# Other order tables and another start for a one-core transformer kernel

## What is computed

```python
h = _L0_tok_ref(x, L0_tok_W)                   # patches times a matrix
h = jnp.concatenate([h, txt], axis=1)
h = h + _L0_attn_ref(_layernorm(h), ...)       # softmax over tokens, circular correlation (by DFT), projection
h = h + _L0_ffn_ref(_layernorm(h), ...)        # 192 -> 768, gelu, 768 -> 192
h = h + _L1_attn_ref(_layernorm(h), ...)       # attention over own 324 and 196 shared tokens
h = h + _L1_ffn_ref(_layernorm(h), ...)        # four experts take the 162 best tokens each, then an attention
                                               # over 324 tokens beside a gelu layer, and the results are gated
```

## Time and profile before

| what | value |
|---|---|
| median of 3 executions | 2089.15 us (2087.38 to 2093.47) |
| the profiled execution | 2096.61 us, span 2094.9 us |
| PE busy | 1871.9 us, 89% of the span |
| DVE / ACT / POOL busy | 60% / 53% / 14% |
| mean granted TensorE clock | 0.965 of full speed |

### The profile page before, as it was taken

How to read it: one execution, slowest core, us unless ns; L and a number is a source line. 1 busy time by engine, 2 the same in 40 slices (tenths; PEclk the granted TensorE clock), 3 DMA queues, 4 the chain that set the end, 5 groups by cost and what they waited for, 6 DMA issues and landing times. The chain is left out here.

```text
span 2094.9 us, 41506 instructions
## 1 busy us (share of the span) xinstructions
PE 1871.9 (89%) x11904; PEld 1260.5 (60%) x11904; DVE 1247.5 (60%) x3509; ACT 1110.8 (53%) x2583; POOL 289.3 (14%) x441
## 2 busy tenths in 40 slices
PE   3788998998998998998998997868999999999996
PEld 2565665675665675665675664435666666666664
DVE  2256566666566566666676674535767666666563
ACT  1244555555554555555555554445556565666663
POOL 4201111111111111111111110100100011001000
PEclk9799999999999999999999998879999999999998
DMA  4202212212212212212212202202433334333331
GB/s 151 68 16 58 69 32 71 64 32 74 61 32 67 64 36 69 67 34 69 65 36 69 68 27 76 75 17 80 103 100 90 87 93 119 82 101 101 100 86 36
DMA packets 161303, 143.61 MB, mean 69 GB/s; under 512 B 32284, under 2 KB 136488, under 8 KB 161064
## 3 DMA queue, kind: packets, MB, share of 16 engines
q1 hardware_dynamic: 157448, 136.69, 24.1%
q0 software_dynamic: 2304, 4.79, 1.0%
q10 hardware_dynamic: 1440, 0.75, 0.1%
HBM read 82.79 MB, written 50.16 MB: 63 GB/s over the span
## 5 line engine op out<-in xcount | busy, mean ns | idle before, releaser
L944 ACT ACTIVATE prob<-sps 108x324 f32<-108x324 f32 x1536 | 621.3, 439 | 506.6 <-PE sps L1356 470.3
L1214 DVE TENSOR_REDUCE mxh<-mps 108x1 f32<-108x324 f32 x1152 | 519.7, 489 | 319.2 <-PE mps L1390 315.4
L1356 PE MATMUL sps<-qpack,kpack 128*108 128x324 bf16 x1536 | 436.3, 318 | 33.5 <-ACT prob L944 25.6
L1390 PE MATMUL mps<-kpack,qpack 96*108 96x324 bf16 x1728 | 391.1, 296 | 46.7 <-DMA kpack<-scr_k 28.9
L1356 PEld LDWEIGHTS sps<-qpack,kpack 128*108 128x108 bf16 x1536 | 189.7, 127 | 228.2 <-ACT prob L944 163.0
L1371 PE MATMUL aps<-prob,v 128*32 128x324 f32 x3072 | 320.0, 460 | 2.4 <-DVE gmall L1202 1.1
L1390 PEld LDWEIGHTS mps<-kpack,qpack 96*108 96x108 bf16 x1728 | 215.8, 131 | 175.8 <-issue 57.6
L1342 PE MATMUL lin<-yT,w 128*128 128x324 f32 x576 | 184.0, 450 | 18.3 <-ACT g L844 14.1
L1214 DVE TENSOR_REDUCE mxs<-mps 108x2 f32<-108x392 f32 x288 | 160.0, 555 | 53.9 <-PE mps L1390 53.7
L1342 PEld LDWEIGHTS lin<-yT,w 128*128 128x128 f32 x576 | 102.4, 192 | 64.4 <-issue 33.2
L767 POOL CAST piece<-rest 128x324 bf16<-128x324 f32 x96 | 43.7, 456 | 700.2 <-DVE rest L1045 695.9
(11 more groups left out here) (150 smaller groups left out, 2354.8 us busy)
## 6 DMA issues: line engine op xcount, KB each, us to landing
qpack<-scr_q SPq DMA_DIRECT2D x96, 243.0 KB, 3.2
kpack<-scr_k SPq DMA_DIRECT2D x96, 121.5 KB, 3.3
scr_q<-piece SPq DMA_DIRECT2D x32, 243.0 KB, 2.9
scr_k<-piece SPq DMA_DIRECT2D x32, 243.0 KB, 3.5
kpack<-scr_k SPq DMA_DIRECT2D x96, 81.0 KB, 3.1
bc<-rec_d SPq DMA_DIRECT2D x112, 60.8 KB, 2.4
scr_q<-piece SPq DMA_DIRECT2D x32, 162.0 KB, 3.3
scr_q<-piece SPq DMA_DIRECT2D x64, 81.0 KB, 3.0
```

What stands on the lines that cost most here:

```text
L944: nc.scalar.activation(prob[0:rows, n % NP, :], sps[0:rows, n % 2, 0:N], ACT.Exp, scale=SCALE).then_inc(att.exped.sem, 1)
L1214: nc.vector.tensor_reduce(dst, src, AX.X, ALU.max, negate=True).then_inc(att.mps.free["dve"].sem, 1)
L1356: mm(sps[0:rows, n % 2, 0:N], kpack[:, 4 * q + n % 4, k * att.rows:k * att.rows + rows], qpack[:, 4 * q + n % 4, :], start=True, stop=True ...
L1390: done = mm(bank[0:P, s * SC:s * SC + k1 - k0], qpack[0:6 * D, 4 * q + hd, t * P:(t + 1) * P], kpack[0:6 * D, 4 * q + hd, k0:k1], start=Tr ...
```

## The change

It has four parts. (1) `ORDER_1` is another order of the same words: 60 `s`, 15 `a`, 54 `m`, 3 `r`, 7 `p` and the same steps; in `ORDER_2` only the nine `p` have moved. (2) The line that places the words of `two` in the turn has other constants. (3) The starting values of the semaphores are added by ACT instead of SP; the loads are split, so that PE's first step and DVE's copy of `ident` wait for two loads only (`loads_tok`), and PE's first `zv` waits for the other five. (4) POOL does 4 of the 13 memsets first; the other 9 come after its first root, at `ln1_1` of i = -2.

```diff
 ORDER_1 = (
-    "a ln2_1 m m m s v_0.0 s ln2_3 s s v_0.1 m s m p v_1.0 s recip s",
-    "t2_0 m a s t2_1 m m s",
-    "m s a s hid0 m hid1 pack2",
-    "m hid2 shared hid3 s m s hid4 m m p norm a m",
-    "hid5 m s s m proj4_0.0 m den proj4_0.1 s spread0 spread1 proj4_1 s s ln4_0 a s ln4_1 r ln4_2 hx s",
-    "out_0.0 m m out_0.1 a m p out_0.2 ln4_3 out_0.3 m out_1.0 m out_1.1",
-    "s m s ln3_0 tok.0 s tok.1 m m s hab t4_0 t4_1 ln3_1 s m a m log m s t5_0",
-    "exp p m s s ln3_3 t5_1 s m s a",
-    "s prob m t3_0 hc m s t3_1 a ln1_0 m qk0 m m qk1 s s qk2 s s ln1_1 p r",
-    "s todram s prt a s s",
-    "a s t1_0 t1_1 s s ln1_3 zv s",
-    "val_0.0 zs val_0.1 s val_1 pack0 zt s m m m dft_0.0 m p pack1 m a m s m dft_0.1 m s m dft_1.0 m m",
-    "m dft_1.1 s of s a s",
-    "s m s m m a s inv_0.0 s m p s m s m s",
-    "inv_0.1 inv_1.0 inv_1.1 s r proj_0.0 proj_0.1 proj_1 xload s ln2_0 a",
+    "den ln2_1 m m m spread0 a s s v_0.0",
+    "m s m s m p s v_0.1 s ln2_3 recip m m v_1.0 s s t2_0 a pack2 s",
+    "s a m s t2_1 s m m m s shared hid0 hid1",
+    "m m hid2 p hid3 hid4 hid5 norm m s m a s",
+    "m spread1 proj4_0.0 proj4_0.1 m proj4_1 s out_0.0 ln4_0 s out_0.1 out_0.2 ln4_1 s out_0.3 ln4_2 a s s r",
+    "m out_1.0 p m m m out_1.1 ln4_3 m a t4_0 ln3_0 t4_1 m s m s tok.0",
+    "ln3_1 m s tok.1 m m s t5_0 ln3_3 hab m s a",
+    "hc t5_1 log s exp m m t3_0 t3_1 m prob hx s s m m qk0 m ln1_0 s qk1 s qk2 m s s a s ln1_1 todram s prt s s s p",
+    "r a s",
+    "a s s t1_0 t1_1 ln1_3",
+    "a",
+    "s zv s val_0.0 val_0.1 zs p s val_1 m s m s zt m m m s dft_0.0 m p s m dft_0.1 m m s m dft_1.0 m m m s dft_1.1 m a",
+    "of pack0 s s a m s s m",
+    "m s a s inv_0.0 m s",
+    "s pack1 inv_0.1 s inv_1.0 inv_1.1 r a p s proj_0.0 xload proj_0.1 proj_1 ln2_0 s",
 )
...
-                while rest and (0.1 + 0.9 * rest[0][0] / len(two.items)) * len(one.items) <= n and not held(rest[0][1]):
+                while rest and (-0.039 + 1.111 * rest[0][0] / len(two.items)) * len(one.items) <= n and not held(rest[0][1]):
...
+        TOKENS = [(w_tok, A["w_tok"]), (ident, A["ident"])]
+        FIRST = [(w_a, A["w_a"]), (w_v0, A["w_v0"]), (dft, A["dft"]),
...
         @block.sync
         def _(sp):
-            for s in primed:
-                sp.sem_inc(s.sem, s.at(s.first, 0) + s.passed)
+            for dst, src in TOKENS:
+                sp.dma_start(dst.ap(), src).then_inc(loads_tok.sem, 16)
...
+            FEW = ((of[64:KP, :, :, :], 0.0), (aT[KC:KP, :, :], 0.0), (aT[KC:KC + 1, :, :], 1.0), (minus_half[:, :, :], -0.5))
...
                         reciprocal_roots(number(name) - 1, j)
+                        if name == "ln1" and isinstance(i, int) and i == -2:
+                            pool.wait_ge(root_known[0].sem, root_known[0].at(j, 1))
+                            memsets(REST, len(FEW))
...
         @block.scalar
         def _(act):
+            for s in primed:
+                act.sem_inc(s.sem, s.at(s.first, 0) + s.passed)
...
-            pe.wait_ge(loads_first.sem, 16 * NFIRST)
+            pe.wait_ge(loads_tok.sem, 16 * len(TOKENS))
             pe.wait_ge(setup_dve.sem, SETUP_DVE - 1)
             pe.wait_ge(setup_pool.sem, 3)
...
                 elif name == "zv":
+                    if isinstance(i, int) and i == -2:
+                        pe.wait_ge(loads_first.sem, 16 * NFIRST)
```

More of the change, by code:

```diff
@@ L58 @@
 ORDER_2 = (
[2 rows of a table removed]
+    "a m m m v_0.0 s m den m s m pack2 v_0.1 m m s scale0 v_1.0 m scale1",
+    "spread0 s m s m m s s qk0 s spread1 s recip p p p qk1 r a s s todram qk2",
     "a s",
[1 row of a table removed]
+    "m m m s s m out_0.0 p yload p s m m m s a s s norm m m m out_0.1",
     "out_0.2 m s m out_0.3 s s pack0 a",
[4 rows of a table removed]
+    "r out_1.0 s out_1.1 s s a",
+    "fin_0.0 s s m a s s m p",
+    "p fin_0.1 s s a m s s m fin_1.0 s m s m m s hold end p hid0 hid1 pack1 m m m s tload hid2 m m",
+    "a p hid3 r hid4 hid5",
 )
@@ L500, in comes_first @@
             return att is two and isinstance(j, int) and j == 0
-        loads_first, loads, setup_dve, setup_pe, setup_act, setup_pool, sc_first, sc_rest, sc_mid, sc_pieces, sc_scr, sc_pack = (
-            signal(n, 0) for n in ("loads_first", "loads", "setup_dve", "setup_pe", "setup_act", "setup_pool", "sc_first",
+        loads_tok, loads_first, loads, setup_dve, setup_pe, setup_act, setup_pool, sc_first, sc_rest, sc_mid, sc_pieces, sc_scr, sc_pack = (
+            signal(n, 0) for n in ("loads_tok", "loads_first", "loads", "setup_dve", "setup_pe", "setup_act", "setup_pool", "sc_first",
                                    "sc_rest", "sc_mid", "sc_pieces", "sc_scr", "sc_pack"))
@@ L541, in build @@
         block = ctx.enter_context(nc.Block())
-        FIRST = [(w_tok, A["w_tok"]), (ident, A["ident"]), (w_a, A["w_a"]), (w_v0, A["w_v0"]), (dft, A["dft"]),
+        TOKENS = [(w_tok, A["w_tok"]), (ident, A["ident"])]
+        FIRST = [(w_a, A["w_a"]), (w_v0, A["w_v0"]), (dft, A["dft"]),
                  (idft, A["idft"]), (w_p0, A["w_p0"])]
@@ L729, in _, with memsets @@
             load_x(0)
[L730 to L735, removed]
-                if n:
-                    pool.wait_ge(setup_pool.sem, n)
-                nc.gpsimd.memset(x, value).then_inc(setup_pool.sem, 1)
-            pool.wait_ge(setup_pool.sem, MEMSETS_POOL)
+            FEW = ((of[64:KP, :, :, :], 0.0), (aT[KC:KP, :, :], 0.0), (aT[KC:KC + 1, :, :], 1.0), (minus_half[:, :, :], -0.5))
+            REST = ((xS[KC:KP, :, :], 0.0), (v1[:, :, :, :], 0.0), (kpack[KC:KP, :, :], 0.0), (yA[KC:KP, :, :], 0.0),
+                    (v1[:, 0:KT1 - 1, :, D:D + 1], 1.0), (v1[0:LAST1, KT1 - 1, :, D:D + 1], 1.0),
+                    (kpack[6 * D:6 * D + 3, :, :], 1.0), (yA[KC:KC + 1, :, :], 1.0), (bc[:, :, :], 1.0))
+            def memsets(sets, done):
+                for n, (x, value) in enumerate(sets):
+                    if n + done:
+                        pool.wait_ge(setup_pool.sem, n + done)
+                    nc.gpsimd.memset(x, value).then_inc(setup_pool.sem, 1)
+                pool.wait_ge(setup_pool.sem, done + len(sets))
+            memsets(FEW, 0)
+            assert len(FEW) + len(REST) == MEMSETS_POOL
             def shared_pieces():
@@ L984, in shared_keys @@
             def shared_keys():
-                dve.wait_ge(loads_first.sem, 16 * NFIRST)
+                dve.wait_ge(loads_tok.sem, 16 * len(TOKENS))
                 nc.vector.tensor_copy(identb[:, :], ident[:, :]).then_inc(setup_dve.sem, 1)
```

## The result

The changed kernel takes 2008.13 us (median of 4 executions, 2005.51 to 2012.99), the kernel before beside it 2091.31 us (4 executions): a ratio of 0.960, with a 95% interval of 0.957 to 0.963. A second set of executions gave 2008.00 beside 2090.75. The profiled execution took 2008.32.

A forecast was written before the change was run, and what follows sets the result against it. PE, busy 89% of the span, was taken to bound the kernel by its waits. Start -9.5, full iterations -36.4, `p` +2, i = 14 -1 and turn -6 summed to -50.9 us: median 2038 us, range 2014 to 2072.

The forecast's parts named there:

- The start: Up to the first `proj`: earlier loads and POOL's moved memsets, taken as hidden, gain 9.5 us.
- Rival 3: The start gives only 4 of its 9.5 us, by memsets beside DVE or ACT's additions: 2043 us; chance 0.05.
- (a): Full iteration, `qk2` to first `m` of group 0: more words and a shorter chain over DRAM, -2.2 us.
- (b): Full iteration, `dft_1.1` to `inv` and `inv` to `proj`: more words fill PE's waits for DVE, -1.6 us.
- (d): Full iteration, before `t2`: `ln2_3` waits longer for POOL's root behind six maxima instead of three, +0.4 us.
- (c): Full iteration, `hid0` to `hid5` unbroken by `s`: two table loads instead of four, fewer waits for gelus, -0.5 us.
- (e): Full iteration, before `out_0.0`: new wait for DVE's `ha`, +1.0 us; likewise `t3_1` and `qk2` behind DVE's reading, +0.3.
- rival 2: The order gives more, as waits before `t2` and `out_0.0` hide in later ones: 3.6 us per iteration, 2024; chance 0.12.
- The +2 for the `p`: Full iterations with `p`: moved among DVE's busier work, they cost 0.4 us in 5 iterations, +2 us.
- i = 14: Last iteration before the turn: front's words are dead, PE idles on the same chain, and its shortening gives -1 us.
- The turn behind it: Turn without `den`: `two`'s maxima ahead of `recip` at i = 16, -1 us; `hid2` to `hid5` together at i = 15, -3.
- The second pipeline: Only `p` moved, with 0.7 us idle per iteration: 0 gain, bounds -4 to +3 us.

The follow-up runs named there:

- start_only: The kernel before with only parts 3 and 4 (ACT adds semaphore values, split loads, memsets behind the root): 2090.22 us, ratio 1.000.
- memsets_later: The changed kernel with POOL's seven short moved memsets behind `ln1_3` and the two of `kpack` behind `zs`: 1997.83 us, ratio 0.955.
- image_first: memsets_later, with SP also waiting for the first image and text before it issues the five loads of `FIRST`: 1999.71 us.
- max18_early: The changed kernel with the 18th maximum of group 2 ahead of `qk0`'s rest on DVE again: 2042.29 us, ratio 0.976.
- ha_behind_max: The changed kernel with the 18th maximum of group 1 ahead of `proj4_0.1`, so that DVE's addition `ha` stands behind it: 2013.86 us.
- order1_only: The kernel before with only the new `ORDER_1`: 2025.42 us, ratio 0.970.
- rule_old: The changed kernel with the old constants in the rule that merges the two tables in the turn: 2022.27 us.
- order2_old: The changed kernel with the nine `p` of `ORDER_2` in their old places: 2014.27 us.
- after_again: The changed kernel run once more, unaltered, as a yardstick in a second set: 2008.00 us, ratio 0.960.

## Why the prediction was wrong, step by step

The direction and the main mechanism were right, the sum 37 us short between the profiles (50.9 forecast, 88.3 measured).

- **The start, -9.5: wrong.** It gave 0.2 us up to the first `proj`: 9.3 are missing. In start_only it gave 1.0 there (44.83) and nothing in the time. The step that failed is "the nine memsets moved behind the root: hidden". They run beside DVE's `xn`, and DVE stood. Rival 3, with a chance of 0.05 and a price of 5.5 us, named this mechanism; memsets_later shows it: with the memsets elsewhere the first `proj` starts 7.0 us earlier than before. The sentence that a DVE memset beside a POOL memset shows "no hindrance yet" took one kind of instruction as a witness for another. Its reading was right: DVE's three short memsets take 0.33 us beside POOL's before, and the same 0.33 in the changed kernel, where POOL's have ended at 5.64. `xn` and `zexp` do not keep their time. The Trainium skill (SBUF — State Buffer, "Who interferes with whom") tells of such a lock for DVE's two-port modes, among them those of `tensor_scalar`; the trace agrees, with 8.21 us for 0.96 and 0.89 for 0.38, both `tensor_scalar`, though no row tells in which mode an instruction ran. A smaller miss: PE started at 8.53, not 7.0, since the last text load landed late beside the weights (image_first gives the 7.0, and a first `proj` 9.7 us earlier than before; but from there on the clock took that gain back).
- **(a) -2.2: right** (5.6 to 3.5 us of waits), and so were its two reasons, with other sizes. 1.5 us are more words to fill the same wait; the chain itself gave 0.5 instead of 0.9. Of the 1.6 us of small operations 0.84 reached `rest`, the half that the prediction allowed for; behind `rest` the chain was 0.3 us longer. max18_early shows the mechanism (1.78 us of delay on DVE become 1.77 at `m`), but not that the small operations were worth that much in the change.
- **(b) -1.6: right** (2.7 to 1.1). **(d) +0.4: right** (0.5 to 0.9).
- **(c) -0.5: right in kind, 0.8 in size.** ACT goes on 0.01 to 0.02 us behind each load, so that a load costs it the 1.28 us of its row and no more.
- **(e) +1.0: wrong.** The prediction placed `ha` behind the 18th maximum. The new table has `proj4_0.1`, at which DVE adds the first part of `ha`, *ahead* of that `m`. No wait arises; with `ha` behind the `m` and 2.1 us of words after it, ha_behind_max shows 0.3 us. The small +0.3 was not there either. So the sum per iteration is -2.1 -1.6 -0.8 +0.4 = -4.1 instead of -2.6, beyond rival 2 (3.6), and the 13 iterations between the first reciprocals gave 53.7 us, where the prediction had 13 x 2.6 less 2 for the `p`, 31.8. This is 21.9 of the 37 us. The +2 for the `p` did not come: at a clock of 1.00 the iterations with `p` went from 77.8 to 72.9 us, those without from 78.3 to 74.1.
- **Not counted: i = -1, and most of i = 0, 12.9 us.** Up to the first reciprocal 15.5 us are gained beside the start's 0.2, and the prediction had 2.6 there, for i = 0: it gave the filling iterations none. PE is busy there for only 146.8 of 206.6 us, each wait of the chain is bare (no other word fills it), and the granted clock falls: in windows of 10 us from 50, 80, 90 and 110 us the kernel before had 0.53, 0.66, 0.58 and 0.66. order1_only reaches its first reciprocal 17.5 us earlier, with 10.8 us less of PE busy time for nearly the same matmuls and 6.7 us less of idle time: the one is the clock, the other are waits. The rows, before and order1_only:

```profile
0.00:206.60 206.60, 146.81 (x773) 103.12 (x777) 85.26 (x238) 65.32 (x153) 51.27 (x65) 0.89 0.26 74
```

```profile
0.00:189.10 189.10, 135.99 (x767) 97.57 (x768) 84.40 (x240) 62.18 (x149) 51.21 (x65) 0.95 0.27 79
```

  Which words of the order do it was not tried.
- **i = 14, -1 forecast, -7.8 measured in its interval: mis-sized.** "The shorter chain gives -1" left out that i = 14 has most of a full iteration's waits: PE's idle time falls by 4.1 us there, as in a full iteration, and its busy time by 3.6, with a clock of 0.91 instead of 0.88. The order does it, since order1_only has 75.6 us too. `den` ahead of `pack2` lies in the same interval: DVE's wait behind it fell by 1.0 (4.77 to 3.75), where the prediction gave -2 to PE.
- **The turn behind it, -4 forecast (-6 with `den`), -5.5 measured: near by luck.** The order made these two intervals 2.4 us longer (order1_only). "At i = 16 `two`'s maxima come ahead of `recip`: -1" was the whole of what the rule does there, and it was priced without reading the row: the reciprocal stood 13.31 us, and PE 2.9 us beside it before (4.2 in rule_old). The profiles put the rule at 7 to 8 us of idle time and 8.5 to 13 in all, the timed executions at 6 to 14. The table loads of the turn went from 11 to 7; what they are worth was not tried.
- **The second pipeline, 0 forecast, -6.0 measured**, outside its bound of -4: the `p` words (4.7 of it in order2_old). "0.7 us of idle time per iteration" was read in an iteration without `p`, 41.0 us long; those with `p` were 42 to 43 and had the room.

The range failed because its low end came from rival 2 alone, with the start at full price: terms for stages that had been called "0", or not been looked at (fill, i = 14 and turn, `p`), had no part in it, and they made 12.9 + 6.2 + 6.0 = 25.1 us.

## What to carry to other kernels

Work moved on an engine off the critical path can still stand beside another engine's instruction: ask what runs *at that moment* on its partner, and witness it with the same kind of instruction. When a loop body gets shorter, cost the filling and emptying iterations by their own rows, since every wait is bare there and the clock can fall behind it. And compare an experiment that undoes one part with the kernel before as well: in the new order the part may cost more than it did in the old one. And before a term is called small, read the row of the very wait that it moves.

## What the runs showed of the hardware

The granted clock decides more than expected. It fell to its lower level (1.2 of 2.4 GHz, a granted clock of 0.5) behind stretches in which PE had stood or worked sparsely. In full iterations of the changed kernel it fell once at most, 0.2 to 2.1 us behind the end of PE's wait for `pack0`, and such an iteration takes 75.5 us instead of 74.1. Windows of one in after_again:

```profile
463.00:467.00 4.00, 2.66 (x20) 2.06 (x18) 1.36 (x5) 2.38 (x8) 0.00 (x0) 1.00 0.77 202
467.00:470.00 3.00, 3.00 (x14) 2.18 (x12) 1.51 (x5) 0.51 (x2) 0.00 (x0) 0.55 0.00 0
```

In other iterations the same wait was followed by no fall: the eleven waits with a fall were 1.3 to 2.4 us long, the fifteen without one 0.9 to 1.7. Of the 13 full iterations 5 and 6 had one in the two profiles of the changed kernel, 3 in the kernel before; at about 1.5 us each that is as much as some edits of a table are worth, and what decides whether one comes is open. The turn varies by the clock too: with the same words and nearly the same idle time of PE (32.7 and 32.2 us) its last two intervals took 146.3 us at a clock of 0.91 in image_first and 150.9 at 0.85 in the changed kernel.
